# Making a third of a position table on GpSimd: TensorE and ScalarE take 257 of its 384 columns

## The reference

```python
rel = jnp.arange(t)[None, :] - jnp.arange(t)[:, None]
rel_pos = jnp.clip(rel + ATT_SPAN, 0, 2 * ATT_SPAN - 1)      # ATT_SPAN = 128
p2c_pos = jnp.clip(-rel + ATT_SPAN, 0, 2 * ATT_SPAN - 1)
scores = jnp.einsum('bhqd,bhkd->bhqk', Q, K) * scale
c2p = jnp.einsum('bhqd,shd->bhqs', Q, pos_key) * scale
c2p = jnp.take_along_axis(c2p, rel_pos[None, None, :, :], axis=-1)
p2c = jnp.einsum('bhkd,shd->bhks', K, pos_query) * scale
p2c = jnp.take_along_axis(p2c, p2c_pos[None, None, :, :], axis=-1)
scores = scores + c2p + jnp.swapaxes(p2c, -1, -2)
probs = jax.nn.softmax(scores, axis=-1)
```

## Time and profile before

| | us |
|---|---|
| runs (three) | 9773.81, 9779.72, 9788.48; median 9779.72 |
| the profiled execution | 9794.44 |
| its span in the profile | 9792.7 |
| attention loop in it, first to last exp | 662.8 to 3855.9 |
| busy over the span: PE, DVE, ACT, Pool | 8291.0, 8405.7, 5593.9, 4994.4 |

### The profile page before, as it was taken

One profiled execution on the slowest core, in us unless ns is written; L12 is line 12 of the kernel. 1 busy time (PEld: TensorE's weight loads), 2 busy tenths in 40 slices (PEclk: granted clock), 3 DMA queues, 4 the chain that ended last, 5 costly groups with the idle time before them and its releaser, 6 DMA issues. The chain is left out here.

```text
span 9792.7 us, 173946 instructions
## 1 busy us (share of the span) xinstructions
PE 8291.0 (85%) x48396; PEld 4749.3 (48%) x48396; DVE 8405.7 (86%) x13204; ACT 5593.9 (57%) x9153; POOL 4994.4 (51%) x4685
## 2 busy tenths in 40 slices
PE   4559999999999998499688888888688888888599
PEld 2236766766666666366333333333233333333366
DVE  4558888888888887699599999999599999999799
ACT  1237777777777776133366666665466565565233
POOL 0000000000000000188499999999599999999487
PEclk7779999999999999799899999999899999999799
DMA  5568898888888888311122211122122222212111
GB/s 180 195 221 280 281 283 281 279 283 279 280 282 281 280 282 253 102 43 42 66 77 79 79 71 62 68 77 79 54 84 88 88 88 88 83 71 73 45 42 40
DMA packets 1171859, 1447.34 MB, mean 148 GB/s; under 512 B 81354, under 2 KB 1051610, under 8 KB 1138688
## 3 DMA queue, kind: packets, MB, share of 16 engines
q1 hardware_dynamic: 1171520, 1444.17, 44.8%
HBM read 880.81 MB, written 564.60 MB: 148 GB/s over the span
## 5 line engine op out<-in xcount | busy, mean ns | idle before, releaser
L1960 POOL TENSOR_TENSOR mb_bx<-mb_dtu,mb_bc 128x512 f32<-128x512 f32 x2048 | 2661.3, 1323 | 8.6 <-DVE mb_hs L2060 8.2
L2203 PE MATMUL mb_y_ps<-mb_g,ident 128*128 128x512 f32 x4096 | 2188.1, 641 | 462.4 <-DVE mb_g L2020 238.4
L2247 ACT ACTIVATE mb_dA<-mb_dt,mb_a_neg 128x512 f32<-128x512 f32 x2048 | 1400.7, 688 | 1622.1 <-DVE mb_hs L2060 1073.1
L1396 POOL MEMSET f_magic<- 128x1 f32 x2 | 0.2, 98 | 3657.1 <-POOLq L127 3657.1
L2203 PEld LDWEIGHTS mb_y_ps<-mb_g,ident 128*128 128x128 f32 x4096 | 763.3, 199 | 1645.7 <-issue 726.3
L1007 ACT ACTIVATE at_tab<-at_e_ps 128x384 f32<-128x384 f32 x2064 | 1012.1, 490 | 814.8 <-PE at_e_ps L924 814.4
L1061 DVE TENSOR_REDUCE at_nmax<-at_s_ps 128x1 f32<-128x1024 f32 x1025 | 1255.3, 1225 | 35.1
L940 PE MATMUL at_pT_ps<-ident,at_probs 128*128 128x128 f32 x8192 | 1116.3, 279 | 102.5 <-ACT at_probs L1012 84.1
L1012 ACT ACTIVATE at_probs<-at_s_ps,at_nmax 128x1024 f32<-128x1024 f32 x1025 | 1140.8, 1113 | 62.5 <-DVE at_nmax L1061 39.3
L940 PEld LDWEIGHTS at_pT_ps<-ident,at_probs 128*128 128x128 f32 x8192 | 894.4, 141 | 406.4 <-ACT at_probs L1012 377.7
L2020 DVE TENSOR_TENSOR mb_g<-mb_hs,mb_bc 128x512 f32<-128x512 f32 x1472 | 995.1, 676 | 37.8 <-PE mb_y_ps L2203 36.6
(11 more groups left out here) (236 smaller groups left out, 14185.0 us busy)
## 6 DMA issues: line engine op xcount, KB each, us to landing
at_tables<-at_tab SPq DMA_DIRECT2D x1032, 384.0 KB, 4.0
at_skew<-at_tables SPq DMA_DIRECT2D x1030, 256.0 KB, 3.2
mb_bc<-mb_bc_rows SPq DMA_DIRECT2D x256, 1024.0 KB, 6.5
at_skew<-at_tables SPq DMA_DIRECT2D x773, 128.0 KB, 3.5
at_opnd<-at_q_st SPq DMA_DIRECT2D x130, 210.0 KB, 4.5
at_opnd<-at_kl_st SPq DMA_DIRECT2D x130, 210.0 KB, 4.7
at_opnd<-at_kr_st SPq DMA_DIRECT2D x130, 210.0 KB, 4.7
at_q_st<-st_parts SPq DMA_DIRECT2D x96, 256.0 KB
```

The source lines that it names most:

```text
L1960: pool.tensor_tensor(bx[:, s % RINGS, :], dtu[:, c, :], bc[:, 0, n, :], ALU.mult).then_inc(s_bx, 1)
L2203: nc.tensor.matmul(y_ps[:, c % 2, :], ident[:, :], g[:, s1 % RINGS, :], start=False, stop=(n == STATE - 1)).then_inc(s_y, 1)
L2247: nc.scalar.activation(dA[:, s % DA_RING, :], dt[:, c, :], ACT.Exp, scale=a_neg[:, c, n:n + 1]).then_inc(s_dA, 1)
```

## The change

Both ends of a table meet an edge: in one third of its 384 columns the difference against one edge is the difference against the other edge plus a constant, which is a column of its own. TensorE now makes 257 columns (256 differences against one edge, and the one column of edge against edge), ScalarE copies 257, and a new program on Pool makes the missing 128 by adding the edge column, broadcast, to the middle 128. tab gets two more columns for the edge columns (386 instead of 384), and the stored 384 columns start at the second. SP's store waits for Pool's signal s_far in place of s_tab; PE still waits for s_tab. The differences are prepared with 257 columns, key_ext and query_ext have 260.

```diff
+DIFF = 2 * SPAN + 1
+DIFFERENCES = (((0, 2 * SPAN, SPAN - 1, EXT - 2), (2 * SPAN, 1, EXT - 2, 0)),
+               ((1, 2 * SPAN, SPAN, 0), (0, 1, 0, EXT - 2)))
...
-                    for j, (to, width, first) in enumerate(DIFFERENCES[k]):
-                        at = ends[j if k == 0 else 1 - j]
+                    for to, width, first, at in DIFFERENCES[k]:
...
-        tab = sb("tab", [P, NE, BAND])
+        tab = sb("tab", [P, NE, BAND + 2])
...
-                ge(sp, s_tab, n1 * NE + 2 * t + 2)
+                ge(sp, s_far, n1 * NE + 2 * t + 2)
...
-                             tab[:, 2 * t:2 * t + 2, :]).then_inc(s_tw[part], 16)
+                             tab[:, 2 * t:2 * t + 2, 1:1 + BAND]).then_inc(s_tw[part], 16)
...
-                mm = nc.tensor.matmul(e_ps[:, 0:BAND], opnd[0:ROWS, u1, side, t * P:(t + 1) * P],
-                                      ext[:, bass.ds(n1 % HEADS, 1), :].rearrange("r a u -> r (a u)"),
+                mm = nc.tensor.matmul(e_ps[:, 0:DIFF], opnd[0:ROWS, u1, side, t * P:(t + 1) * P],
+                                      ext[:, bass.ds(n1 % HEADS, 1), 0:DIFF].rearrange("r a u -> r (a u)"),
...
+        @block.gpsimd
+        def _(pool):
+            def make_far(n1, e):
+
+                to, step = (1 + 2 * SPAN, 0) if e % 2 else (1, 1 + BAND)
+                ge(pool, s_tab, n1 * NE + e + 1)
+                pool.tensor_tensor(tab[:, e, to:to + SPAN], tab[:, e, 1 + SPAN:1 + 2 * SPAN],
+                                   tab[:, e, step:step + 1].to_broadcast([P, SPAN]), ALU.add).then_inc(s_far, 1)
+
+            for e in range(NE):
+                make_far(0, e)
...
-                nc.scalar.activation(tab[:, e, :], e_ps[:, 0:BAND], ACT.Copy).then_inc(s_tab, 1)
+                at = 0 if e % 2 else 1 + SPAN
+                nc.scalar.activation(tab[:, e, at:at + DIFF], e_ps[:, 0:DIFF], ACT.Copy).then_inc(s_tab, 1)
...
-    split = dram("split", (2, 3, D, BAND), BF16)
+    split = dram("split", (2, 3, D, DIFF), BF16)
...
-        key_ext = sb("key_ext", [ROWS, HEADS, BAND], BF16)
-        query_ext = sb("query_ext", [ROWS, HEADS, BAND], BF16)
+        key_ext = sb("key_ext", [ROWS, HEADS, DIFF + 3], BF16)
+        query_ext = sb("query_ext", [ROWS, HEADS, DIFF + 3], BF16)
```

More of the change, by code:

```diff
@@ L329, in third_steps @@
     return nc.vector.tensor_tensor(lo, left, mid, ALU.subtract)
-DIFFERENCES = (((0, SPAN, SPAN - 1), (SPAN, 2 * SPAN, SPAN - 1)),
-               ((0, 2 * SPAN, SPAN), (2 * SPAN, SPAN, 2 * SPAN)))
+DIFF = 2 * SPAN + 1
+DIFFERENCES = (((0, 2 * SPAN, SPAN - 1, EXT - 2), (2 * SPAN, 1, EXT - 2, 0)),
+               ((1, 2 * SPAN, SPAN, 0), (0, 1, 0, EXT - 2)))
 def position_tables(nc, relT, relT_back, w_pk, w_pq, b_pk, b_pq, scale, split_dram,
@@ L352, in position_tables @@
         full = sb("full", [P, 2, DC, EXT])
-        band = sb("band", [P, 2, DC, BAND])
-        parts = sb("parts", [P, 2, DC, 3, BAND], BF16)
-        left = sb("left", [P, BAND])
+        band = sb("band", [P, 2, DC, DIFF])
+        parts = sb("parts", [P, 2, DC, 3, DIFF], BF16)
+        left = sb("left", [P, DIFF])
         zeros = sb("zeros", [P, table_dram.shape[2], SPAN])
@@ L383, in _ @@
                 for j, s in enumerate(which):
-                    sp.dma_start(ext[j * DK:(j + 1) * DK, :, :],
+                    sp.dma_start(ext[j * DK:(j + 1) * DK, :, 0:DIFF],
                                  split_dram[k, s].rearrange("(h r) u -> r h u", r=DK)).then_inc(s_back, 16)
@@ L790, in attention_loop @@
         s_val = [sem(f"val_loaded{u}") for u in range(2)]
-        s_E, s_tab = sem("table_done"), sem("table_kept")
+        s_E, s_tab, s_far = sem("table_done"), sem("table_kept"), sem("far_made")
         s_tw = [sem(f"table_stored{k}") for k in range(len(PARTS))]
@@ L998, in _, with pair @@
             sum_lanes(GROUPS - 1, end)
+        @block.gpsimd
[7 more added lines that the diff above has]
+                make_far(0, e)
+            def pair(j):
+                for u in range(2):
+                    for e in range(NE):
+                        make_far(j * 2 + u + 1, e)
+            pair(0)
+            if heads // 2 > 1:
+                with pool.Fori(1, heads // 2) as j:
+                    pair(j)
         @block.scalar
```

## The result

The kernel after takes 9794.24 us (median of 20 runs, 9783.33 to 9807.29), the kernel before 9779.51 (20 runs): ratio 1.0014, interval [1.0007, 1.0020], 14.7 us slower. The forecast was 9782 us and no change that a measurement tells.

The account below looks back on a forecast made before the run. Compute (24.84 us a head) and SP's DMA round (24.91) were taken as nearly level bounds. With the round at 24.99 against 24.95, 127 heads gave +5 us, -3 ahead of the loop: +2 on 9779.72, 9782 us, range 9690 to 9855.

Parts of the forecast that it names:

- a gain in one circle is stopped by the other: Attention loop: compute (24.84 us a head) and SP with the DMA queue (some 24.9) nearly level, so one gain alone is stopped.
- (a): Table matmul on PE, 384 to 257 columns: 0.053 us less each, 2064 times, 109 us of PE time.
- (b): ACT's table copy, narrowed to 257 columns: 0.106 us less each, 219 us of ACT time.
- (d): Pool's 16 additions a head: some 0.46 us each, 7.4 us of 24.95, so Pool keeps up.
- (c): Compute circle in the loop: 0.08 to 0.1 us less a q-tile, some 0.65 a head, to 24.2 us.
- Rival 1: Attention loop: SP's round gives way and compute sets the pace, 0.75 us a head faster, 9682 us; chance 0.25.
- the round: SP's four skew-load groups a head, each waiting for earlier stores to land: 24.91 us, 24.99 after, setting the pace.
- (e): SP's store waits for Pool some 0.6 us after the table copy, hidden behind the first store's landing: costed at nothing.
- (f): Table stores from rows moved 4 bytes and 1544 bytes apart: 0.08 us a head, bounds nothing and 0.62.
- (g): Ahead of the loop: 16 tables made one after another, -2 us, and preparation, -1 us.
- over 100 operand waits: Sign in the loop: PE's waits for the operand rise from 18 to over 100, on a head's first table matmul.
- Rival 3: Loop: Pool and DVE hold each other up, 0.9 us a head, some +115 us, 9895 us; chance 0.04.

Follow-up runs that it names:

- e2: Kernel after with table stores cut to the middle 128 of 384 columns: 9761.19 us, ratio 0.9970 to the kernel before.
- e9: Kernel after with two of four skew-load groups (tiles 0 and 1, 6 and 7) issued behind the next store: 9748.85 us, ratio 0.9965 to before.
- e1: Kernel before with table stores cut to the middle 128 of 384 columns: 9793.61 us, ratio 1.0004 to before.
- e10: Kernel before with two of four skew-load groups (tiles 0 and 1, 6 and 7) issued behind the next store: 9777.98 us, ratio 0.9996.
- e3: Kernel before plus one 128-column Pool addition per table into a spare tile, SP's store waiting for it: 9794.33 us, ratio 1.0003.
- e5: Kernel before with only tab's rows moved (386 columns a row, stored 384 starting at the second): 9793.54 us, ratio 1.0009.
- e4: Kernel after without Pool's additions beyond the first head, SP's store waiting for ACT's copy as before: 9806.84 us, ratio 1.0014 to before.
- e6: Kernel after with tab rows of 512 columns, the stored part starting at column 64: 9796.36 us, ratio 1.0008 to before.
- e11: Kernel before plus three 128-column Pool additions per table ahead of the signal SP's store waits for: 9798.10 us, ratio 1.0016.
- e12: Repeat of the unmodified kernel after in a later set of runs on one chip: 9797.63 us, ratio 1.0016 to before.

## Why the prediction was right

The forecast was 9782 us, in a range of 9690 to 9855; the time is 9794.24. The range is wide, and its chances were nearly even (0.35 faster, 0.34 the same, 0.31 slower), so a time inside it proves little. What the experiments bear out is the mechanism on which the sum rests.

**The bound.** That a gain in one circle is stopped by the other is shown from three sides: the loop after takes 24.96 us a head with an undisturbed head at 24.62; with fewer bytes (e2) or another order of waits (e9) the same instructions take 24.63 and 24.64; and in the kernel before the same two edits free only 0.1 us a head (e1 24.85, e10 (3842.4 - 661.2)/128 = 24.85).

**(a), (b), (d).** Right: -53 ns, -105 ns (forecast -53, -106), Pool 397 ns (0.46 estimated by a straight line through wider forms).

**(c)** failed in size. "I take 0.08 to 0.1: some 0.65 us a head, so compute alone would go at 24.2" came out as 0.22 us, 24.62. The step had the right brake, "the maximum ends only 0.12 us before the exp", and then let most of the gain through it. The trace after shows the brake: exps that wait for DVE rose from 126 (31.4 us) to 492 (152.9 us), half of all q-tiles. Over some 1010 q-tiles that is 0.12 us more each, which with the 0.03 gained makes up nearly all of the 0.16 shed. What in turn held DVE back, for which the prediction allowed 0.05 to 0.1 us a q-tile, the runs do not take apart. Rival 1, had it come true, would have given 42 us and not 95; e9 against before is 35. The forecast did not rest on this term, since the round was taken as the bound. That was the forecast's good fortune: had the round given way, a term three times too large would have been the whole forecast.

**(e)** right within what can be told: 0 expected, e3 1.0003. **(f)** 0.08 us a head, 10 us: e5 (+5 us in the median) fits it and does not prove it. **(g)** -3 us ahead of the loop; the first exp came 5.8 us earlier in this pair of traces.

**The round itself** was taken as 24.91 and grew to 24.99 in the sum; the traces have 24.96 and 25.02 for the loop. That "no link of the round holds a wait for compute" went a little too far: in the kernel before, some 10 of about 417 groups did not wait for a landing, and SP waited 36 times (13 us in 2600) for PE's scores ahead of the operand loads. And the forecast of over 100 operand waits was too high: 67 and 83, with the skew waits beside them.

**The 14.7 us.** The forecast had +2, and 0.11 + 0.16 + 0.04 for a loss of more than 20. The measured loss is smaller than the 20 us that the prediction thought could be told, but twenty runs of each kernel do tell it. Which of the edits makes the small loss stays open. Without the Pool wait it is there (e4), with the rows back in place it is not clearly gone (e6), and each edit alone in the kernel before is too small to tell (e3 +0.03%, e5 +0.09%). The traces hold one pointer. The longest link of the round, from the store of tile 7 to the group that waits for it, takes 5.00 us on average before and 5.11 after; it is 5.21 in e4, where the second store goes out soonest, and 4.93 and 4.86 in e3 and e11, where it goes out later. So stores issued closer together may land later. Single heads of one trace do not show this relation, and no run tests it. What the runs leave is a loop of 24.96 us a head in the first trace after and of 25.02 in that of e12 (658.8 to 3861.9 us), against 24.95 before; compute's gain cannot pay for it while the round is the bound. Rival 3 is excluded: DVE's maximum takes 1225 ns and its copies 681 in both kernels, with 16 additions a head on Pool beside them.

## What to carry to other kernels

Follow the queue that issues DMAs round its own circle (issue, landing, next issue) and set it beside the circle of the engines; where the two are level, as here, taking work from an engine buys nothing, however much busy time it removes (118 us of ACT and 66 of PE in 2000 us). Such a circle can be opened by order alone: moving the wait for a landing behind one more independent issue was worth nothing that can be told by itself (e10) and released the 0.3% that the other edit had earned. And when an engine gets less to do, ask how much slack its partner at the same meeting point has: of 0.16 us a q-tile that the matmul and the copy shed here, 0.03 was left after the exp had begun to wait for DVE more often.

## What the runs showed that I had not expected

A kernel whose DMA engines are 0.88 busy, and whose queue waits for a landing in front of nearly every group, had room for all its bytes at a 1.2% faster pace (e9: 0.90 busy, 284 GB/s); a DMA share of 0.88 was no sign of a full queue. And three Pool additions (398 ns each) in front of every table's signal made SP wait only 212 us more for tables in 2600 us, and 192 us of that came back as shorter landing waits (e11).
